# A last group of half size in a routed MLP: leftover sequences of a short route come last, y of the group before stays in PSUM

## The reference

```python
out_nr  = gelu(x @ w1_nr + b1_nr) @ w2_nr + b2_nr            # condition 0
out_tsr = gelu(x @ w1_tsr + b1_tsr) @ w2_tsr + b2_tsr        # condition 1
h = gelu(x @ w1_sr + b1_sr)                                  # condition 2, 256 -> 512
h = gelu(h @ w2_sr + b2_sr)                                  # 512 -> 256
out_sr = h @ w3_sr + b3_sr                                   # 256 -> 256
out = where(c == 0, out_nr, where(c == 1, out_tsr, where(c == 2, out_sr, 0)))
y = x + out
mu, var = mean(y), mean((y - mu) ** 2)                       # over the 256 features
return (y - mu) * rsqrt(var + 1e-5) * gamma + beta
```

## Time and profile before

| what | value |
|---|---|
| median of three runs | 109.97 us |
| the profiled execution | 109.8 us, its span 108.1 us |
| TensorE busy | 88.2 us, 82% |
| VectorE busy | 75.7 us, 70% |
| GpSimd busy | 66.6 us, 62% |
| ScalarE busy | 64.6 us, 60% |
| GpSimd, gamma or beta over two tiles (128x512) | 1.26 us |
| GpSimd, `root` | 1.04 us |
| ScalarE, one z tile | 0.59 us |
| instruction DMA queues | 20 packets, 0.25 MB |
| mean granted TensorE clock | 0.954 |

### The profile page before, as it was taken

The page is one execution under the profiler, slowest core; times in us unless marked ns, Lnnn a source line. Parts: engine busy times, 40 slices in busy tenths (PEclk is TensorE's granted clock), DMA queues, the critical chain, the costliest instruction groups (busy, mean ns, idle before and its releaser), DMA issues.

```text
span 108.1 us, 1785 instructions
## 1 busy us (share of the span) xinstructions
PE 88.2 (82%) x523; PEld 77.5 (72%) x523; DVE 75.7 (70%) x194; ACT 64.6 (60%) x105; POOL 66.6 (62%) x79
## 2 busy tenths in 40 slices
PE   0259999999999999999999999999999999900000
PEld 0157778868889888898998989989989899800000
DVE  5579086562655096729989989899898979799200
ACT  0685239995995046895967959689688574070000
POOL 6337910029777304006769987879878888989800
PEclk9999999999999999999999999999999999996555
DMA  0995996000498990000004031040130400105191
GB/s 4 282 300 171 241 345 220 0 0 3 150 296 297 414 378 27 0 6 0 0 6 194 3 129 50 9 194 0 70 130 6 194 0 11 56 0 191 30 287 62
DMA packets 5572, 12.85 MB, mean 119 GB/s; under 512 B 800, under 2 KB 2864, under 8 KB 5552
## 3 DMA queue, kind: packets, MB, share of 16 engines
q0 software_dynamic: 2736, 9.44, 24.1%
q1 hardware_dynamic: 2668, 2.89, 9.1%
q10 hardware_dynamic: 148, 0.27, 0.7%
HBM read 8.40 MB, written 4.72 MB: 121 GB/s over the span
## 4 chain that ended last, share of the span: by engine, by line
PE 68%; POOL 13%; DMA 4%; DVE 4%; issue 2%; POOLq 1%; ACTq 1%; ACT 1%; DVEq 0%
PE ps_f L819 19%; PE ps_a L760 8%; PE ps_x L744 8%; PE ps_a L761 8%; PE ps_a L765 8%; PE ps_f L868 4%; POOL xs L391 4%; DMA bias_rows<-L_cond_b_sr_dram 4%; PE ps_f L806 3%; POOL xs L386 3%; POOL rstd L376 3%; POOL out_dram L399 2%; PE ps_b L862 2%; PE ps_b L860 2%; PE ps_b L861 2%
## 5 line engine op out<-in xcount | busy, mean ns | idle before, releaser
L386 POOL TENSOR_TENSOR xs<-xs,gamma_b 128x768 f32<-128x768 f32 (+1 forms) x8 | 14.3, 1787 | 6.1 <-ACT xs L459 5.9
L455 ACT ACTIVATE f_hi<-ps_a,bias_cols 128x512 fp32r<-128x512 f32 x16 | 11.0, 688 | 9.7 <-PE ps_a L862 4.7
L760 PE MATMUL ps_a<-x_hi,w_lo 128*128 128x512 f32 x40 | 16.6, 414 | 0.2 <-issue 0.2
L819 PE MATMUL ps_f<-wf_hi,f_hi 128*128 x64 | 15.9, 282 | 0.0
L819 PE MATMUL ps_f<-wf_lo,f_hi 128*128 x64 | 15.9, 281 | 0.0
L761 PE MATMUL ps_a<-x_hi,w_hi 128*128 128x512 f32 x40 | 15.7, 393 | 0.0
L347 POOL DMA_INDIRECT xs<-x_dram,load_idx x11 | 11.4, 1037 | 6.4 <-DVE load_idx L576 3.5
L376 POOL TENSOR_TENSOR rstd<-var_eps,half 128x4 f32<-128x4 f32 x9 | 9.4, 1040 | 9.4 <-DVE var_eps L636 9.3
L459 ACT ACTIVATE xs<-xs,shift,rstd 128x256 f32<-128x256 f32 x23 | 12.1, 593 | 4.2 <-POOL shift L380 4.2
L456 ACT ACTIVATE ps_a<-ps_a,bias_cols 128x512 f32<-128x512 f32 x22 | 14.3, 652 | 0.0
L391 POOL TENSOR_TENSOR xs<-xs,beta_b 128x768 f32<-128x768 f32 (+1 forms) x8 | 14.2, 1776 | 0.1
(11 more groups left out here) (137 smaller groups left out, 190.7 us busy)
## 6 DMA issues: line engine op xcount, KB each, us to landing
w_raw<-L_cond_w_sr_dram SPq DMA_DIRECT2D x2, 512.0 KB, 4.4
wf_raw<-L_cond_w_sr_dram SPq DMA_DIRECT2D x1, 256.0 KB
w_raw<-L_cond_w_tsr_dram SPq DMA_DIRECT2D x1, 256.0 KB, 5.2
w_raw<-L_cond_w_nr_dram SPq DMA_DIRECT2D x1, 256.0 KB, 5.5
wf_raw<-L_cond_w_tsr_dram SPq DMA_DIRECT2D x1, 256.0 KB, 5.7
wf_raw<-L_cond_w_nr_dram SPq DMA_DIRECT2D x1, 256.0 KB, 5.8
out_dram<-xs ACTq DMA_DIRECT2D x4, 64.0 KB, 3.0
out_dram<-xs SPq DMA_DIRECT2D x4, 64.0 KB, 3.0
```

What stands on the lines that cost most here:

```text
L386: nc.gpsimd.tensor_tensor(tiles, tiles, spread(gamma_b, n), ALU.mult).then_inc(gam_pool, 1)
L455: nc.scalar.activation(hi, bank, ACT.Gelu, bias=bias)
L760: nc.tensor.matmul(dst, w1_lo[:, kt, cols], xh[:, kt, :], start=(kt == 0), stop=False)
L819: return nc.tensor.matmul(ps[:, b, t * H:(t + 1) * H], stationary[:, kt, (2 * b + t) * P:(2 * b + t + 1) * P], weights[:, bass.ds(f_at + k ...
```

## The change

The whole-size group that a short route (TSR or NR) would end with is left out where at most four sequences are left over, and these make a half group of 256 tokens (two tiles, `HTT` = 2), which comes behind all whole groups. There is at most one such group: if TSR has one, NR rounds up as before. Two new classes name it, `HALF_TSR` and `HALF_NR`. `SLOTS` becomes 10, and `GROUPS` = 11 counts the half group.

On VectorE the order work changes: the steps against which counts are compared start at 4 for TSR, the sequences past TSR's whole groups get a place far away, and the class table is made from six kinds. A second row index (`half_load_idx`, `half_store_idx`) is made for rows of 2 KB, by one more small product on TensorE. The half group is gathered by its own indirect DMA, the last one.

The end of the program for an engine is either `half(s)`, where group s is a half group, or `finish(s - 1)` as before. The half block in detail, for half group g: TensorE does layer 1 over 256 columns, the last layer of g-1 into `ps_f`, and the last layer and x of g into one bank of `ps_x`. VectorE adds x to `ps_f` in place, so y of g-1 stays in PSUM, and normalizes it by fused passes as the last group before. GpSimd has no pass over group g-1; `store_part` does not wait for `o_pool` there.

The core of the diff:

```diff
+        def each_step(eng, cls, step, half, finish):
+            def end(s):
+                with eng.If(cls[s] < EMPTY):
+                    half(s)
+                with eng.Else():
+                    finish(s - 1)
...
                     with eng.If(cls[s] > NR):
                         if s == MIN_GROUPS:
-                            finish(s - 1)
+                            end(s)
                         else:
-                            with eng.If(cls[s - 1] < EMPTY):
-                                finish(s - 1)
+                            with eng.If(cls[s - 1] < HALF_TSR):
+                                end(s)
...
+            for first, n, base_at in ((0, TSR, 0), (TSR, 1, HPER), (NR, ROUTES - NR, 0)):
+                nc.gpsimd.iota(steps_of[:, first:first + n, :], [[0, n], [PER, PER]], base=base_at, ...
...
+            nc.vector.tensor_scalar(tsr_far[:, :], key[:, :], float(NR - TSR), FAR, ALU.is_equal, ALU.mult)
...
+            nc.vector.tensor_scalar(past_tsr[:, :], over[:, TSR, :], 0.0, tsr_far[:, 0:1], ALU.is_equal, ALU.mult)
+            nc.vector.tensor_scalar(passed[:, 0, :], full[:, :], rank[:, 0:1], None, ALU.is_le)
+            nc.vector.scalar_tensor_tensor(out=passed[:, 1, :], in0=steps_of[:, 0, :], scalar=rank[:, 0:1],
+                                           in1=past_tsr[:, :], op0=ALU.is_le, op1=ALU.mult)
...
+            nc.vector.tensor_copy(cnt[:, :], counts_pt).then_inc(dve_step, 1)
...
+            chain(nc.vector.tensor_scalar(kinds[:, HALF_TSR:HALF_TSR + 1], kinds[:, TSR:TSR + 1], float(PER),
+                                          cnt[:, TSR:TSR + 1], ALU.mult, ALU.is_lt))
+            chain(nc.vector.tensor_scalar(nr_slack[:, :], ...))
+            chain(nc.vector.tensor_scalar(over_nr[:, :], ...))
+            chain(nc.vector.tensor_reduce(kinds[:, NR:NR + 1], over_nr[:, :], AX.X, ALU.add))
+            chain(nc.vector.tensor_scalar(kinds[:, HALF_NR:HALF_NR + 1], ...))
-            for r in range(ROUTES):
+            for r in range(ROUTES + 2):
                 nc.vector.tensor_scalar(ended[:, :, r], slot_id[0:1, :], ends[:, r:r + 1], None, ALU.is_ge)
...
+            nc.vector.tensor_scalar(near[:, :], nth[:, :], FAR / 2, None, ALU.is_lt).then_inc(dve_step, 1)
+            nc.vector.tensor_tensor(own_kind[:, :], own[:, :], kinds[:, 0:ROUTES], ALU.mult).then_inc(dve_step, 1)
...
+            chain(nc.vector.tensor_reduce(own_full[:, :], own_kind[:, :], AX.X, ALU.add))
+            chain(nc.vector.scalar_tensor_tensor(out=half_place[:, :], in0=own_full[:, :], ...))
+            nc.vector.scalar_tensor_tensor(out=half_row_at[:, :], in0=half_row_place[:, :], ...
+                                           ).then_inc(half_place_done, 1)
...
+            def dve_half(g):
+                for m in range(2):
+                    low(ps_a[m][:, 0, 0:HTT * P], f[:, m, 0:HTT * P], f_l[:, m, 0:HTT * P], ...)
+                dve.wait_ge(f_ready, 2 * (g - 1) + 2)
+                nc.vector.tensor_tensor(ps_f[...], ps_f[...], xs[g - 1][:, :, :], ALU.add).then_inc(y_done, 1)
+                dve.wait_ge(y_done, g)
+                for t in range(TT):
+                    nc.vector.bn_stats(stats[:, t, :], next_tile(t)).then_inc(bn_done, 1)
+                moments(g - 1, ps_b)
+                dve.wait_ge(mv_done, g)
+                times_gamma_first(g - 1, next_tile, TT, u_next)
+                dve.wait_ge(f_ready, 2 * g + 1)
+                for t in range(HTT):
+                    nc.vector.bn_stats(stats[:, t, :], half_tile(t)).then_inc(bn_done, 1)
+                moments(g, ps_b, HTT)
+                gamma_beta_shared(g - 2)
+                root_and_beta(g - 1, next_tile, xs[g - 1], TT, u_next)
+                dve.wait_ge(mv_done, g + 1)
+                times_gamma_first(g, half_tile, HTT, u_last)
+                root_and_beta(g, half_tile, xs_half, HTT, u_last)
...
+            def half_group(g):                         # TensorE
+                pe.wait_ge(x_lo_done, upto_x(g))
+                ... half_first(TSR or NR, g)           # layer 1 over 256 columns
+                last_layer(g - 1)
+                last_layer_and_x(g, route, 1)          # one bank of ps_x
...
+            pe.wait_ge(half_place_done, 1)
+            nc.tensor.matmul(half_rows_pt, half_row_at[:, :], seq_ones[:, 1:2], start=True, stop=True)
...
+            def pool_half(g):                          # GpSimd
+                root(g - 1)
+                times_gamma(g - 2, 2, TT)
+                plus_beta(g - 2, 2)
+                root(g, HTT)
+                scatter(g - 2, False)
+                pool.wait_ge(o_dve, 2 * (g + 1))
+                nc.gpsimd.indirect_dma_start(out=half_out_rows, ..., in_=xs_half[...]).then_inc(stored[g], 16)
...
+            def act_half(g):                           # ScalarE
+                for m in range(2):
+                    gelu(ps_a[m][:, 0, 0:HTT * P], f[:, m, 0:HTT * P], ...)
+                normed_shared(g - 2)                   # z of tiles 2 and 3 into ps_z, of 0 and 1 in place
+                store_part(act, seq_regs, taken_regs, g - 1, PER // 2, False)
```

More of the change, by code:

```diff
@@ L15 @@
 EPS = 1e-5
-NONE, SR, TSR, NR, EMPTY = range(5)
+NONE, SR, TSR, NR, HALF_TSR, HALF_NR, EMPTY = range(7)
 ROUTES = 4
@@ L79, in build_cond_mlp @@
         over_before = sb("over_before", [B, ROUTES, PER])
+        cnt = sb("cnt", [B, ROUTES])
+        tsr_far = sb("tsr_far", [B, 1])
+        past_tsr = sb("past_tsr", [B, PER])
+        over_nr = sb("over_nr", [B, PER])
+        nr_slack = sb("nr_slack", [B, 1])
+        kinds = sb("kinds", [B, ROUTES + 2])
+        own_kind = sb("own_kind", [B, ROUTES])
+        own_full = sb("own_full", [B, 1])
+        half_place = sb("half_place", [B, 1])
+        half_row_place = sb("half_row_place", [B, P])
+        half_row_val = sb("half_row_val", [B, P])
+        half_row_at = sb("half_row_at", [B, P])
+        half_load_idx = sb("half_load_idx", [P, 1], I32)
+        half_store_idx = sb("half_store_idx", [P, 1], I32)
+        near = sb("near", [B, 1])
         base = sb("base", [B, 1])
@@ L115, in build_cond_mlp @@
         stats = sb("stats", [P, TT, 6])
[L116 to L118 removed]
+        neg_mean = sb("neg_mean", [P, GROUPS, TT])
+        var_eps = sb("var_eps", [P, GROUPS, TT])
+        rstd = sb("rstd", [P, GROUPS, TT])
         shift = sb("shift", [P, SLOTS, TT])
@@ L222, in load_classes @@
         def load_classes(eng, name):
-            regs = [eng.alloc_register(f"{name}{s}") for s in range(SLOTS)]
-            eng.load(regs, cls_tab[0:1, 0:SLOTS])
+            regs = [eng.alloc_register(f"{name}{s}") for s in range(GROUPS)]
+            eng.load(regs, cls_tab[0:1, 0:GROUPS])
             return [eng.snap(r, min_val=0, max_val=EMPTY) for r in regs]
@@ L365, in _ @@
                 gather(s)
+            pool.wait_ge(half_idx_done, 2)
+            nc.gpsimd.indirect_dma_start(
+                out=xs_half[:, :, :].rearrange("p t h -> p (t h)"), out_offset=None, in_=half_x_rows,
+                in_offset=bass.IndirectOffsetOnAxis(ap=half_load_idx[:, 0:1], axis=0)).then_inc(half_loaded, 16)
             pool.wait_ge(bcast_in, 16 * 2)
@@ L372, in _, with root @@
             pool.reg_mov(last_row, NROWS - 1)
-            def root(g):
+            last_half_row = pool.alloc_register("last_half_row")
+            pool.reg_mov(last_half_row, HNROWS - 1)
+            def root(g, n=TT):
                 pool.wait_ge(mv_done, g + 1)
-                nc.gpsimd.tensor_tensor(rstd[:, g, :], var_eps[:, g, :], half[:, :], ALU.pow).then_inc(rstd_step, 1)
+                nc.gpsimd.tensor_tensor(rstd[:, g, 0:n], var_eps[:, g, 0:n], half[:, 0:n], ALU.pow
+                                        ).then_inc(rstd_step, 1)
             def shifted(g):
@@ L542, in _ @@
             nc.vector.tensor_scalar(before[:, :], route_id[:, :], key[:, 0:1], None, ALU.is_gt)
+            nc.vector.tensor_scalar(tsr_far[:, :], key[:, :], float(NR - TSR), FAR, ALU.is_equal, ALU.mult
+                                    ).then_inc(dve_step, 1)
+            step[0] += 1
             dve.wait_ge(own_done, 1)
@@ L571, in _ @@
                                            ).then_inc(place_done, 1)
-            chain(nc.vector.tensor_reduce(groups[:, :], over[0:1, :, :], AX.X, ALU.add))
-            chain(nc.vector.tensor_tensor_scan(ends[:, :], groups[:, :], zeros[:, :], 0.0, ALU.add, ALU.add))
+            nc.vector.tensor_reduce(kinds[:, 0:NR], over[:, 0:NR, :], AX.X, ALU.add).then_inc(dve_step, 1)
+            nc.vector.tensor_copy(cnt[:, :], counts_pt).then_inc(dve_step, 1)
+            step[0] += 2
             dve.wait_ge(rows_ps, 1)
@@ L655, in middle, with times_gamma_first, root_and_beta @@
                 moments(g, ps_z)
+            def times_gamma_first(g, tile, n, done):
+                for t in range(n):
+                    nc.vector.scalar_tensor_tensor(out=tile(t), in0=tile(t), scalar=neg_mean[:, g, t:t + 1],
```

(13 more changed lines are left out.)

284 lines of the change are left out of this document (189 added, 95 removed).

## The result

| kernel | median (range), us | against before |
|---|---|---|
| before | 109.94 (109.8 to 109.99), 4 runs | 1 |
| after | 108.00 (107.74 to 108.37), 4 runs | 0.9826 [0.9808, 0.9844] |

The change gains 1.9 us, not the 3.7 that I forecast: 108.0 lies outside 105.0 to 107.6, on the slow side. The profiled execution took 108.14 (109.8 before), its span 106.4 (108.1). Where the two traces part is read in three places.

What follows compares the result with a forecast made beforehand. It took TensorE up to the last group, the norm of the last two groups and the stores to count. Release -3.6, stores -0.4 and front +0.35 sum to -3.65 from 109.8: 106.2 us written, range 105.0 to 107.6.

Steps and rivals of the forecast that it cites:

- Part 1: TensorE's tail: products would end at 90.0 in place of 94.3, without being the bound of the end.
- Part 2: VectorE's tail becomes the bound: group 7's stores released at 97.55 in place of GpSimd's 101.21, -3.6 us.
- Part 3: GpSimd and ScalarE in the tail lie beside the bound: rstd(7) and rstd(8) have slack 3.0 and 1.8.
- Part 4: Group 7's stores at the end: release to last wait 5.3 us in place of 5.7, -0.4 (-1.4 to 0).
- Rival C: End of kernel: the half scatter lands last, at 103.95, 1.05 behind the stores; 107.25 us, 11%.
- Part 5: The front: sixteen added VectorE instructions and one more TensorE product cost +0.35 us (0 to +1.0).
- the cover: Front: the 2.67 us VectorE idled before x_lo of group 0 hides the 2.3 of added order work, nearly used up.
- rival B: Front: order work at 0.3 per instruction breaks through its cover, some 1.3 us reaching TensorE; 107.5 us, 12%.
- The way out: SyncE's exit behind the last wait: more code to jump over might add 0.45 to 0.9 us; taken as 0.
- rival D: SyncE's exit: more stops in the code on the way out, +0.9, 107.1 us, 6%.
- E: Front: slower than before, VectorE's order work above 0.45 per instruction; at 0.5, 110.6 us; 4%.
- F: Last group isn't made a half group on this input, only the front's +0.35 remains: 110.3 us, 1%.

Runs made afterwards that it cites:

- e10: Changed kernel with the half group kept, but y of the last whole group in SBUF and ScalarE's z and GpSimd's passes as before: 109.28 us.
- e8: Changed kernel with group 6's gamma, beta and scatter moved earlier inside the half block: 107.2 us.
- e5: Changed kernel with group 7 stored by one indirect scatter on GpSimd in place of eight stores: 107.26 us.
- e11: Changed kernel with the edits of e2, e8 and e5 together: 106.13 us.
- e2: Changed kernel with VectorE's `bf_parts` moved from ahead of x_lo of group 0 to the end of step 0: 107.65 us.
- e6: Changed kernel with SLOTS cut to 8, the whole groups this input needs: 107.5 us.
- e16: Changed kernel with the early scatter of group 6 (e8) and SLOTS = 8 together: 106.66 us.
- e4: Changed kernel without the eight stores of group 7; the half group's scatter stays: 106.48 us.
- e3: Changed kernel without the half group's scatter, its 256 tokens not stored: 107.56 us, spread from 107.05 to 108.1.
- e14: Kernel before with an unused tensor of 32 bytes per partition ahead of `xs`: 110.38 us.
- e7: Kernel before with SLOTS cut to 9, the groups this input needs: 108.71 us.
- e12: e11 with the half group's row index made later and its small product at the head of step 1: 106.48 us.

## Why the prediction was wrong

The direction, the mechanism and the order of the end were right; two terms were too small, and one thing had no term.

**Part 1, TensorE.** Its last product ends at about 91.5 where 90.4 was forecast; 0.7 of that is the later front and pace, the rest was not traced. It was, as said, not the bound.

**Part 2, the release, -3.6.** Right. In its own frame the chain was 0.3 better than worked out (14.35 against 14.67), since 4.34 instead of 4.73 passed from y of group 6 to the first `low`. e10 shows from the other side that GpSimd's share of group 7 was what held the end.

**Part 3, GpSimd and ScalarE.** Both roots came in time. But scatter(6) was noted as "ends 97.6", as if that were its end, when its data only start to move at 99.1: this is the slip behind the next term.

**Part 4, the stores, -0.4. This step failed.** Release to last wait was 98.25 to 105.2 = 6.95, not 5.3: +1.65. I argued that "only the end of group 6's scatter and 128 KB of the half" would run beside the stores. In fact all of its 512 KB did. Group 7 has seven real sequences now, and an issue for an empty place moves nothing (256 KB went over SyncE's queue, 192 over ScalarE's), so from the first store on 512 + 448 + 128 = 1088 KB had to go out, where before it was 512 + 448 = 960; and the stores waited behind the 512: their first bytes moved 1.8 behind the issue, for 0.9 before. Taking the crowd apart gives 0.8 back by the medians in e8 and in e5, 1.5 with both (e11 against e2), and the unused slots some 0.5 (e6, e16), part of it in the way out. How the 1.65 divides among them is not shown: one scatter in place of eight stores was not tried on the kernel before, which might gain by it too. The half scatter took 5.0 for my 3.1, and 3.2 without the stores (e4). Rival C had the sign (SyncE's long wait at the end is for the half scatter, which I had named as a sign of being wrong) but not the whole mechanism: e3 shows the stores as late without it.

**Part 5, the front, +0.35. This step failed too.** It came to +1.04. Of the 0.69 between, 0.35 is `bf_parts` (e2): I counted the cover of 2.67 against the added instructions alone, at 2.3 where they took 2.71, and did not ask what the moved ones would meet. `bf_parts` moved from 9.51 to 12.06, where it runs beside GpSimd's subtraction for wf_lo, and took 1.0 more. That is the end that rival B named (the cover breaks) by a road that it did not. x_lo started at 14.27, outside my 13.5 to 14.0. That the meeting is the cause of the 2.28 is read from the 18 timelines, which agree without an exception (under e2); no run took the subtraction away. 0.44 is the pace of the products, for which no view of before could give a term (e14 costs the kernel before as much by a shift of 32 bytes; that the same is at work in after is not shown); the two together make 0.79 for 0.69, which leaves 0.1 for the other terms of the front, taken a little too dear.

**The way out and rival D.** From the last wait to the end 1.2 passed, as before: the extra stops that D feared there did not come. But the code was in the account at another place: packets of instructions moved beside the last stores, and without the unused slots after took 0.5 less and before 0.6 to 1.3 less (e6, e7), of which 0.3 in before is an earlier first store. The Trainium skill ("Runtime: NRT & Kernel Launch", section Instruction fetch mechanics) says that a taken branch to a page not held waits for its fetch; the trace agrees as far as the way out shortens from 1.2 to 0.5 with the slots gone from before. **E and F** did not happen.

The sum by measured terms, against before's profiled execution: release -4.0 + 1.04 (y of group 6 at 83.90, then 14.35) = -2.96; from the release on 6.95 for 5.7, +1.25; 109.8 - 2.96 + 1.25 = 108.1; measured 108.14.

## What to carry to other kernels

When an edit shifts a queue, price the old instructions at their new time, too: look at what runs on the neighbouring engines there. Of the DMAs ahead of the last stores, count from when their bytes move, not from when their issue ends, and order the last norms so that the older group's data are gone before the last group's come. Work that is moved out of one path (e12) needs its price at the place that it moves to; and an unrolled slot that this input does not fill still costs at the end.

## What the runs showed of the hardware

- A 2x1024 `SCALAR_TENSOR_TENSOR` on VectorE with its operands in SBUF took 1.27 or 1.28 us beside the issuing of GpSimd's gathers (four profiles), and 2.28 to 2.32 us when a 128x512 GpSimd subtraction of 1.36 to 1.42 us had started 0.14 to 0.18 us ahead of it (14 profiles); it then ended 1.07 or 1.08 us behind the subtraction, as if it had done its work only after it. In e2 GpSimd's next subtraction took 2.27 us beside it, for 1.30 in after.
- 32 unused bytes per partition made the 512-column products of an otherwise unchanged kernel go 0.2335 apart for 0.2275 at the same granted clock, 0.44 us over the stretch from 16 to 42 us. Behind it the two go at the same pace (6.96 and 6.97 us a group).
- A 128 KB indirect scatter of 2 KB rows lands in 3.2 us without the stores (e4), in 3.7 beside the stores when the 512 KB scatter had gone out earlier (e8), and in 5.0 with both.
- Group 7 by eight issues on two queues, seven of which move 64 KB, ended the kernel 0.7 us later than by one indirect scatter of the same rows (after against e5).
- The bytes of group 6's indirect scatter began to move 1.6 us behind the start of its issue (96.50 to 98.1 before, 97.47 to 99.1 after), those of the half scatter in e4, which came next on the same queue, 1.05 us (100.14 to 101.19), and 2.1 us in after, behind the crowd (100.09 to 102.2).
